# Attention past a recurrent scan: from eight batches one by one to two rounds over pairs of batches, and four token tails joined two by two

## The reference

```
def scan_part(x, h, W, b):                 # UGRNN over 256 steps
    m = concat([x_t, h]) @ W + b
    c, g = tanh(m[:, D:]), sigmoid(m[:, :D] + 1)
    h = g * h + (1 - g) * c
x = x + scan_part(x, cond, W0, b0)
def block(x, t_emb, ...):                  # in tangent space of a Poincare ball
    shift, scale, gate (two sets) = split(t_emb @ w_ada + b_ada, 6)
    xm = expmap0(layer_norm(logmap0(x)) * (1 + sc) + sh)
    q, k, v = heads of plin(xm, w_q|w_k|w_v)
    attn = softmax(q k^T / sqrt(8))        # over all 256 keys, no mask
    a = plin(from_heads(expmap0(attn v)), w_o, b_o)
    x = mobius_add(x, expmap0(g_msa * logmap0(a)))
    ff = plin(plin(modulated norm of x, w_f1), w_f2)
    return mobius_add(x, expmap0(g_mlp * logmap0(ff)))
out = x + block(x, cond)
```

## Time and profile before

| | us |
|---|---|
| median of 3 runs | 487.18 (486.27 to 487.44) |
| the profiled execution | 487.77 |
| its span in the trace | 485.5 |
| granted TensorE clock, mean | 0.92 of full |

### The profile page before, as it was taken

How to read it: one execution, slowest core, us unless ns; L and a number is a source line. 1 busy time by engine, 2 the same in 40 slices (tenths; PEclk the granted TensorE clock), 3 DMA queues, 4 the chain that set the end, 5 groups by cost and what they waited for, 6 DMA issues and landing times.

```text
span 485.5 us, 14029 instructions
## 1 busy us (share of the span) xinstructions
PE 364.5 (75%) x5194; PEld 252.9 (52%) x5194; DVE 318.4 (66%) x1939; ACT 215.4 (44%) x963; POOL 141.0 (29%) x295
## 2 busy tenths in 40 slices
PE   2997987977666787668999989988499788745400
PEld 1746674656555665545665756646345455424400
DVE  6444444575886676886575687554823679798984
ACT  2224222323334323335545455546498886644410
POOL 6000000121480022380013084024700342554642
PEclk9999999999999999999999999999689969767565
DMA  7107500020000000000000000000000000000010
GB/s 176 54 1 158 107 3 1 2 46 2 1 2 3 1 2 3 2 2 1 2 3 3 3 1 2 3 2 1 2 3 1 1 2 2 2 22 3 6 38 22
DMA packets 9113, 8.41 MB, mean 17 GB/s; under 512 B 1275, under 2 KB 7693, under 8 KB 9046
## 3 DMA queue, kind: packets, MB, share of 16 engines
q1 hardware_dynamic: 8950, 7.26, 6.5%
q0 software_dynamic: 96, 0.26, 0.2%
HBM read 6.45 MB, written 1.08 MB: 15 GB/s over the span
## 4 chain that ended last, share of the span: by engine, by line
PE 53%; DVE 24%; ACT 12%; issue 5%; POOL 4%; DMA 1%; SPq 0%; DVEq 0%; POOLq 0%; ACTq 0%
PE zb L778 19%; PE tb L883 5%; DVE prod_hi L1388 4%; PE tb L729 4%; PE firsts L926 4%; PE zb L757 4%; ACT state L1141 3%; PE firsts L947 3%; DVE prod_lo L1394 3%; ACT prd L1274 2%; PE firsts L1019 2%; ACT state L1144 2%; PE zb L763 2%; POOL stat L679 2%; PE firsts L778 2%
## 5 line engine op out<-in xcount | busy, mean ns | idle before, releaser
L778 PEld LDWEIGHTS zb<-prod_hi,whh 128*128 128x128 f16 x1920 | 73.5, 106 | 94.5 <-DVE prod_hi L1388 87.0
L778 PE MATMUL zb<-prod_hi,whh 128*128 128x8 f16 x1920 | 90.7, 171 | 40.5 <-DVE prod_hi L1388 39.6
L1141 ACT ACTIVATE state<-zb 128x8 f32<-128x8 f32 x240 | 42.4, 177 | 168.3 <-PE zb L778 168.3
L1388 DVE SCALAR_TENSOR_TENSOR prod_hi<-state 128x16 f16<-128x16 f32 x255 | 47.3, 185 | 97.8 <-ACT state L1144 95.1
L778 PE MATMUL zb<-prod_lo,whh 128*128 128x8 f16 x960 | 63.5, 172 | 2.9 <-DVE prod_lo L1394 1.0
L1394 DVE TENSOR_TENSOR prod_lo<-prod,prod_hi 128x16 f16<-128x16 f32 x255 | 50.7, 199 | 8.7
L778 PEld LDWEIGHTS zb<-prod_lo,whh 128*128 128x128 f16 x960 | 44.4, 107 | 6.8 <-DVE prod_lo L1394 3.6
L588 POOL TENSOR_TENSOR stat<-mv 128x4 f32<-128x4 f32 x4 | 0.8, 205 | 155.8 <-DVE mv L1484 155.8
L1274 ACT ACTIVATE prd<-zb 128x640 f32<-128x640 f32 x64 | 41.1, 713 | 7.1 <-PE zb L998 6.9
L1390 DVE SCALAR_TENSOR_TENSOR prod<-state 128x16 f32<-128x16 f32 x256 | 43.8, 171 | 0.5 <-ACT state L1144 0.5
L1144 ACT ACTIVATE state<-zb 128x16 f32<-128x16 f32 x240 | 42.8, 178 | 0.0
(11 more groups left out here) (331 smaller groups left out, 726.5 us busy)
## 6 DMA issues: line engine op xcount, KB each, us to landing
mod<-ada_rows SPq DMA_DIRECT2D x4, 768.0 KB, 12.3
resid<-in_x_dram SPq DMA_DIRECT2D x6, 128.0 KB, 3.7
ffz<-shift_rows SPq DMA_DIRECT2D x4, 131.0 KB, 3.3
out_dram<-state SPq DMA_DIRECT2D x8, 64.0 KB, 2.1
out_dram<-early SPq DMA_DIRECT2D x8, 64.0 KB, 2.1
yy<-in_L_cond_w_ada_dram SPq DMA_DIRECT2D x1, 384.0 KB
early<-in_L_cond_weight_dram SPq DMA_DIRECT2D x2, 128.0 KB
resid<-in_x_dram POOLq DMA_DIRECT2D x2, 128.0 KB, 3.5
```

The costliest lines, as they stand in the source:

```text
L778: i = pe.matmul(z_bank(t, k)[:, NB * (t % CH):NB * (t % CH) + NB], whh[:, half, p, k, :], src[:, NB * p:NB * p + NB], start=False, stop=Fa ...
L1141: act.activation(r[:, 24:32], z_bank(t, 1)[:, k:k + NB], ACT.Tanh, scale=-1.0 / ZS)
L1388: dve.scalar_tensor_tensor(prod_hi[:, :], r[:, 16:32], 1.0, r[:, 0:16], ALU.add, ALU.mult).then_inc(hi_ready, 1)
```

## The change

Everything up to the scan's end stays, but for the layout of `QT` (now batch by batch, so that queries of chunks 0 to 2 lie in a row) and for the four groups of chunk 2 that stood in the scan.

Past the scan, attention goes in two rounds over pairs of batches, 16 steps each. In round c (2, then 3) the 64 keys of chunk c of the one batch lie on 64 partitions and those of the other batch on the other 64. A step has, for each of four heads, the queries of chunks 0 to 2 against these keys (L950: 32 rows, 64 columns of the array, 192 queries, once for each batch), and the queries of chunk c against the whole earlier key blocks (L959: `kb` 0 in round 2, `kb` 0 and 1 in round 3; 64 queries each). An exp is 128x640 in the first round and 128x896 in the second. The values follow the same shape: L977 (64 rows, 18 columns, 192 queries) and L986 (128 rows, 64 queries). The outputs of the two batches go to the banks `sbk` and `ob`. DVE saves a batch with two additions after the first round (L1582, L1584) and one after the second (L1588).

The tails: two workers in place of four. The large operations stay one by one for each pair; the chains on 128x4 (mobius, ss, artanh, usum, fq, f1) and the norms and powers on POOL are done for two pairs at once, on 128x8. The tails of pairs 0 to 2 share the two `tb` banks, that of pair 3 has the four banks of `zb`. All the tables are new.

```
-QK0 = CH
-QK1 = NC * CH
-QK = QK0 + QK1
+QW = (3 * CH + 2 * CH, 3 * CH + 4 * CH)
+QK = max(QW)
...
-TAIL_BANKS = 3
+TAIL_BANKS = 2
+LAST_BANKS = 4
+PAIRS = ((0, 1), (2, 3))
+NP = NJ * NI
...
-        QT = sb("QT", [P, NJ, 4, NC * P], F16)
+        QT = sb("QT", [P, NB, 4, STEPS], F16)
...
         def diag_o(b):
-            return sbk[:, :]
+            return (sbk, ob)[b % 2]
         def tail_bank(j, user):
-            return (tb[:, 0, :], tb[:, 1, :], ob[:, :])[TURN[j, user] % TAIL_BANKS]
+            if j == NJ - 1:
+                return diag_bank(TURN[j, user] % LAST_BANKS)
+            return tb[:, TURN[j, user] % TAIL_BANKS, :]
...
                 def scores(g, half):
-                    b = g // NI
+                    c, j = 2 + g // NP, g % NP // NI
...
-                    heads = diag_heads(g, half)
-                    for kb in (1, 0):
-                        for i, hg in heads:
-                            rows = slice(STACK * i, STACK * i + STACK)
-                            chunks, cols = (((NC - 1,), slice(0, QK0)),
-                                            (tuple(range(NC)), slice(QK0, QK)))[kb]
-                            ins = pe.matmul(diag_bank(i)[:, cols], KT[rows, hg, b, kb, :],
-                                            q_cols(QT[rows, b // 2, hg, :], b, chunks),
-                                            start=(kb == 1), stop=True, skip_group_check=True)
+                    for i, hg in diag_heads(g, half):
+                        rows = slice(STACK * i, STACK * i + STACK)
+                        for s in range(2):
+                            b, r = 2 * j + s, CH * (s ^ (c & 1))
+                            pe.matmul(diag_bank(i)[r:r + CH, 0:3 * CH], KT[rows, hg, b, 1, r:r + CH],
+                                      QT[rows, b, hg, 0:3 * CH], start=True, stop=True,
+                                      skip_group_check=True)
+                    n = 0
+                    for kb in range(c - 1):
+                        for s in range(2):
+                            for i, hg in diag_heads(g, half):
+                                rows = slice(STACK * i, STACK * i + STACK)
+                                c0 = 3 * CH + CH * n
+                                ins = pe.matmul(diag_bank(i)[:, c0:c0 + CH], KT[rows, hg, 2 * j + s, kb, :],
+                                                QT[rows, 2 * j + s, hg, CH * c:CH * c + CH], start=False,
+                                                stop=True, skip_group_check=True)
+                            n += 1
...
-            def mobius(now, base, T, name, j, sel, pre, dots, x2s):
-                tau, xy, y2, al, den, w = (tmp[:, 1 + j, i, :] for i in range(12, 18))
+            def mobius(now, base, T, name, cols, sel, pre, dots, x2s):
+                tau, xy, y2, al, den, w = (tmp[:, i, cols] for i in range(12, 18))
...
-            tails = [tail(j) for j in range(NJ)]
+            tails = [tail(n) for n in range(len(PAIRS))]
```

More of the change, by code:

```diff
@@ L183, in att_groups @@
             t = tok_base(1) + 52 + 2 * (NI * b + i)
[L184 to L190 removed]
+            out.append((b, i, t if t < tok_base(2) + 26 else t + 8))
     return out
@@ new lines, in work @@
+                    for p, j in enumerate(PAIRS[n]):
+                        yield from at_ticks(now, base + T["vtrans"][p])
+                        pe.wait_ge(v_ready, j + 1)
+                        transposes(j, "vT", T_O[j]).then_inc(vT_ps, 1)
+                        yield from at_ticks(now, base + T["t6"][p])
+                        pe.wait_ge(vT_sb, j + 1)
+                        b = bank(j, "t6")
+                        for c in range(NC):
+                            ins = pe.matmul(b[:, 8 * c:8 * c + LIN], T_OT[j][:, c, :], lin[:, j, :],
+                                            start=(c == 0), stop=True, skip_group_check=True)
+                        ins.then_inc(t6_ps, 1)
+                        yield from at_ticks(now, base + T["g"][p])
+                        products(j, "g", T_OT[j], gw[:, 0:D]).then_inc(g_ps, 1)
@@ L1107, in tail @@
+                    for p, j in enumerate(PAIRS[n]):
+                        yield from at_ticks(now, base + T["gy"][p])
+                        products(j, "gy", T_OT[j], gw[:, D:2 * D]).then_inc(gy_ps, 1)
                 return work
-            tails = [tail(j) for j in range(NJ)]
+            tails = [tail(n) for n in range(len(PAIRS))]
             run(step, [prepare, tokens, attention, *tails])
@@ new lines, in work @@
+                    for p, j in enumerate(pairs):
+                        yield from at_ticks(now, base + T["v"][p])
+                        settle(marks[j])
+                        for c in range(NC):
+                            ins = dve.scalar_tensor_tensor(T_O[j][:, c, :], T_X[j][:, c, :], mean[:, NC * p + c:NC * p + c + 1],
+                                                           mod[:, c & 1, j, 4 * D:5 * D], ALU.subtract,
+                                                           ALU.mult)
+                        ins.then_inc(v_ready, 1)
```

843 lines of the change are left out of this document (398 added, 445 removed), and 6 rows, old and new, of the table scores.

## The result

| | before | after |
|---|---|---|
| median | 486.79 us | 502.77 us |
| ratio, with 95% interval | | 1.0297 (1.0222 to 1.0372) |
| profiled execution, its span | 487.77, 485.5 | 498.33, 496.5 |
| last save of the attention starts | 427.9 | 415.8 |
| from that save's end to the end of DVE's last row | 53.4 | 74.9 |

The range of the four runs is 498.3 to 507.0; the profiled one is the fastest. Ranges and medians in this document hold all runs, but the ratios leave out every run over 1.5% above the fastest of its kernel, so that of a kernel whose clock moves they hold the favourable runs only.

A forecast was written before the change was run, and what follows sets the result against it. No engine was busy over 75%, so chains were taken to set the end: 314.7 scan + 94 attention + 69.6 tails + 5.0 stores = 483.3, plus 2.3 outside, 485.6; less 0.6 for the median, 485.0, range 479 to 493.

The forecast's parts named there:

- Where the attention ends: Attention past the scan: first round 43 us, second 51, together 94, ending at 408.7 instead of 428.6; bounds 86 and 104.
- the 1.5 of the first round: PE time of one first-round attention step: 0.8 us for values plus 0.7 for scores.
- the 1.95 of the second: PE time of one second-round attention step: 1.05 us for values plus 0.9 for scores.
- the 55 us: PE's sum for scores and values of both rounds, 24 + 31 us, same as before; 66 at the upper end.
- (b): Attention slower: 64-row matmuls not side by side, or many short ones delaying PE's next step; 494, partly hidden 491; chance 0.18.
- a change of the tiling mode: PE in attention steps: six mode changes instead of two, 0.1 us each inside the sum; at twice that 13 us more.
- The third stage: Tails from last save to DVE's last row: 62.0 busy + 6.6 idle + 1.0 POOL stalls = 69.6 us; bounds 65 and 75.
- idle time of 6.6: DVE's gaps in the tails: 6.7 us before, 1.2 more for the last norm, 1.3 taken back for extra rows.
- 0.6 more each: POOL's clip and root powers in the tails: extra cost in us of each, with two pairs' rows behind them.
- (c): Slower tail: wide powers, POOL's additions and the second pair's rows all on the path, 75 us, total 490; chance 0.12.
- my 16 of the small operations: DVE in the tails: pairing takes away half of 308 small operations, some 16 us.
- The end on SP: Final stores issued on SP: 5.0 us follow DVE's last row instead of 3.6.

The follow-up runs named there:

- one_batch: Changed kernel without the second batch's 64-row value matmuls in every group but a batch pair's first; 502.58 us in one run.
- hold: Changed kernel plus zero-weight filler matmuls in value steps 0 to 19 and eight where PE waits for the last chunk; median 494.53 us.
- fill_kick: Changed kernel plus one zero-weight filler matmul in each of 32 value steps and eight in a row before the first; median 497.88 us.
- narrow: Changed kernel with POOL's powers of the second shared tail run on half of their columns; median 503.52 us.
- split: Changed kernel with separate tails for pairs 2 and 3, tables of before moved to fit; median 501.81 us.
- old_att: Attention of the kernel before with the changed kernel's shared tails, tables moved; median 504.93 us.
- again: The changed kernel measured once more, nothing altered, for its spread and a second trace; median 501.26 us.

## Why the prediction was wrong

**Where the attention ends** (forecast 94 us past the scan, measured 101.8). The prices of the steps were right at the full clock: 1.55 us for the 1.5 of the first round, 1.90 for the 1.95 of the second, the 32 exps of 128x896 took 27.8 us of ACT for 26. The failing step is that I took them at the full clock for the whole attention. One row that could have told stood in the earlier trace rows, the other in the same trace: the chunk-2 group at 322.71 takes 0.36 + 0.32 us, and the same group at 340.66 takes 0.24 + 0.22. The prediction read the first as "four chunk-2 score matmuls of 64 queries need 0.32 us before the values can start, much more than their columns"; they needed it because the engine was at 1.2 GHz, and the clock column said 1.00 because nothing had been recorded yet.

```profile
340.66 0.31 PE L926 MATMUL firsts<-prd,V 128*18 128x64 f32 x8
340.90 0.28 PE L947 MATMUL zb<-QT,KT 32*128 32x64 f16 x4
```

In the first round PE was busy for 39.4 us where I had 32. The round still took only 45.3 us instead of 43, since the token chain ran beside it. The second round took 56.5 instead of 51: 22.7 us of it at half clock with PE never idle. I had written that a long fall of the clock would make me wrong, since "then the 55 us nearly double", and gave it no chance and no time; with 54 of its 102 us at 1.2 GHz up to 382.7 alone (27.0 and 27.3) it should have been a rival beside (b). Rival (b) named the right engine and 101.8 lies below its 104, but that is luck: its first mechanism, matmuls that don't run side by side, is refuted by one_batch, and the prices of its second, many short ones, didn't appear at the full clock. Twice 0.1 us for a change of the tiling mode isn't needed either: the steps came out at the lower price.

The clock did not stay low for much longer than in before. With the unrecorded part put at half, the stretch from the scan's end to the last save has some 54 us of half clock out of 114 in before and 58 out of 102 now. What differs is what it hits. In before part of that time found PE idle (busy for 4.1 of the 8.3 us from 343.2 to 351.5); in the changed kernel PE was busy for 51.4 of the 54.3 us up to 341.7 and from 355.4 to 382.7, and so pays nearly all of it in time.

What keeps the clock at half there is not shown. It fell at 355.4 behind five steps at the full clock and a wait of 2.1 us, but in hold it fell at 350.6 behind a wait of 1.0. It rose at 341.7 and 382.7 behind 128x128 matmuls of the tokens and transposes, but there were transposes at 371.68 too, with no rise. Eight fillers in a row were followed by a rise both times, 1.2 us behind their end in fill_kick and 1.5 in hold. The Trainium skill ("TensorE: Matmul & The Clock Gate", Part 1) says that the clock follows how busy the engine has been. If busy means that matmuls are running, the rows disagree: 27.24 of 27.30 us busy at half clock here, and 29.2 of 34.2 us at the full clock in before, from 356.8 to 391.0. Which property of these steps matters, no run here isolates.

**The third stage** (forecast 69.6, measured 74.9). The working of the busy time held: 62.0 and 1.0 for POOL's stalls against 62.8. The step that failed is the idle time of 6.6, "behind them DVE has now 8 rows (2.3 us) of two pairs instead of 4; I take 1.3 back for it": measured are 12.1. The sum behind it is 6.7 + 1.2 - 1.3, so the "0.6 more each" of the clip and root powers was put at nothing and 1.3 taken off besides. Nothing came back. The last norm costs 4.03 us (forecast 3.9), but the first one 2.11 and a clip power 1.31, where before had 0.7 and nothing at all. narrow shows 3.5 us of the 12.1 to be the width of the powers, and split, with one chain more, has 2.2 to 4.1 us less idle time. That the rest is fewer independent chains, so fewer rows to put into a wait, fits old_att's 18.8 us and is argued. Rival (c), with a chance of 0.12, had 75 us for this stage with wide powers in its path: it came true in size and, as far as narrow goes, in mechanism.

The two misses add up for the traced run: 7.8 us of attention and 5.3 of tails on a forecast of 485.6 give 498.7, against 498.3.

**What I had not seen.** The new order of the attention makes all pairs ready late. Between about the last save of pair 0 and that of pair 3 DVE has 60.4 us in before and 37.4 in after, and uses 43.6 and 16.0 of them:

```profile
367.50:427.90 60.40, 48.67 (x659) 30.19 (x654) 43.55 (x291) 44.84 (x144) 21.37 (x41) 0.86 0.01 2
```

```profile
378.40:415.80 37.40, 34.50 (x902) 22.31 (x898) 16.01 (x81) 26.08 (x64) 3.87 (x5) 0.91 0.01 3
```

Past the scan DVE's work fell by 10.7 us (117.6 to 106.9, for my 16 of the small operations), its idle time rose by 20. The prediction had this in counts, 361 instructions behind the last save for 303, but not as lost cover. What the attention gains is in large part paid back in the tails, so the forecast gain was 2 us and its sign hung on two terms that were off by 8 and 5 us.

**The end on SP** was right: 5.1 us follow the last row, for 5.0. POOL's addition held DVE as forecast (1.61 us for two rows of 0.61 together). **The spread** was not forecast at all: again moves by 5 us between runs, before by 1.2 in its first four and by up to 3.3 in the later sets. That the changed kernel, with its bound on PE, takes a shift of the clock more fully fits this; it is argued.

## What to carry to other kernels

- Before a price is taken from a row, compare one operation's start-to-start time at several places of the trace. Here the same value records took 0.80 and 0.47 us and the same chunk-2 group 0.68 and 0.46, which were the two clocks, whatever the clock column said before its first recorded change.
- A change that moves the bound onto TensorE takes over its clock as a term of the sum: price every step at both levels, and ask what keeps the clock up. Here a PE that was busy for 27.24 of 27.30 us stayed at half.
- Operations shared between two chains save busy time and can lose cover (here 6.5 us saved and 2 to 4 given back). Count the waits that no other chain fills, and look at a stage's own length: with a clock that moves between runs, the total hid 3.5 us of a stage, and the same tails took 74.9 or 76.7 us. Compare stages at the same clock.

## What the runs showed of the hardware that I had not expected

- PE busy for 27.24 of 27.30 us at a granted 0.50; work added to it made the kernel 5 us faster (501.3 to 496.1). Work taken from it again did not make it faster in the median (498.3).
- Two sets of 64-row value matmuls on the two halves of the rows run side by side almost without cost: 0.45 us for one, 0.47 for both at the full clock (0.77 and 0.80 at half).
- A 128x128 matmul of 512 columns between steps of smaller tiles took 0.32 us at the full clock, where two 512-column matmuls in a row at L1056 start 0.23 apart (392.06 and 392.29).
- POOL's power takes 1.06 and 1.68 us on 4 and 8 columns in before, and 2.99 on 16 in the changed kernel.
- The scan runs at 1.2 GHz from the first recorded change at 82 us on (0.50 from 100 to 300 us in again) with PE busy for 81% of that stretch.
